# State-space units of a decoder kernel: channel blocks two by two, the scan in place in two PSUM banks, and shares of the work on GpSimd and ScalarE

## What is computed

```python
dt = softplus(dt @ dt_proj_w.T + dt_proj_b)              # per token and channel, 512 channels
dA = exp(einsum('bld,dn->bldn', dt, A))                  # 16 states for each channel
u = einsum('bld,bln->bldn', x, Bc) * dt[..., None]
decay = clip(floor(dA * 2**15), 0.0, 32767.0) / 2**15
h = scan(h = decay * h + u)                              # along the 256 tokens
y = einsum('bldn,bln->bld', h, Cc) + x * D
y = (y * silu(z)) @ out_proj_w.T + out_proj_b
```

## Time and profile before

| | |
|---|---|
| median of 3 runs | 2634.4 us (2625.34 to 2636.75) |
| the profiled execution, its own time | 2631.68 us |
| span of the profiled execution | 2629.8 us |
| DVE busy | 1634.4 us (62%) |
| PE busy | 2168.8 us (82%) |
| ACT busy | 1030.7 us (39%) |
| POOL busy | 289.7 us (11%) |
| units, first scan to last | 1242.6 to 2118.6 us, 128 scans |

### The profile page before, as it was taken

One profiled execution on the slowest core, in us unless ns is written; L12 is line 12 of the kernel. 1 busy time (PEld: TensorE's weight loads), 2 busy tenths in 40 slices (PEclk: granted clock), 3 DMA queues, 4 the chain that ended last, 5 costly groups with the idle time before them and its releaser, 6 DMA issues. The chain is left out here.

```text
span 2629.8 us, 31266 instructions
## 1 busy us (share of the span) xinstructions
PE 2168.8 (82%) x11024; PEld 1327.3 (50%) x11024; DVE 1634.4 (62%) x2717; ACT 1030.7 (39%) x1611; POOL 289.7 (11%) x332
## 2 busy tenths in 40 slices
PE   6999999999999988754668887977888778749994
PEld 4666666666666655431323344434444434536662
DVE  6555555555555566447999999999999952120002
ACT  1222222222222222115765867587668712212220
POOL 1111111111111111100000000010000002110005
PEclk8999999999999999867779987988899876559997
DMA  6000100010001000010110111111001120003333
GB/s 219 1 0 17 46 2 0 17 41 8 0 17 41 7 0 0 1 40 33 54 49 23 47 40 38 34 38 37 27 33 55 48 68 30 15 19 100 100 100 112
DMA packets 57469, 102.55 MB, mean 39 GB/s; under 512 B 7828, under 2 KB 39087, under 8 KB 56832
## 3 DMA queue, kind: packets, MB, share of 16 engines
q1 hardware_dynamic: 54272, 93.67, 10.8%
q0 software_dynamic: 3072, 7.28, 0.9%
HBM read 87.10 MB, written 14.94 MB: 39 GB/s over the span
## 5 line engine op out<-in xcount | busy, mean ns | idle before, releaser
L1788 PE MATMUL pa<-arena 128*128 128x512 f32 x512 | 306.4, 728 | 97.7 <-DVE arena L1363 97.5
L1355 DVE TENSOR_TENSOR_SCAN arena<-arena 128x1024 f32<-128x1024 f32 x128 | 292.3, 2284 | 8.4 <-ACT arena L813 8.0
L1576 PE MATMUL po<-arena 128*128 128x256 f32 x1024 | 230.1, 381 | 0.0
L1566 PE MATMUL pa<-arena 128*128 128x512 f32 x512 | 227.9, 598 | 0.8 <-ACT arena L661 0.8
L1788 PEld LDWEIGHTS pa<-arena 128*128 128x128 f32 x512 | 103.4, 221 | 228.8 <-DVE arena L1363 127.5
L676 ACT COPY arena<-po 128x512 f32<-128x512 f32 x64 | 37.5, 586 | 462.6 <-PE po L1531 462.6
L1576 PEld LDWEIGHTS po<-arena 128*128 128x128 f32 x1024 | 191.2, 189 | 31.9 <-issue 3.5
L528 POOL TENSOR_SCALAR arena<-arena 128x2 f32<-128x2 f32 (+1 forms) x92 | 27.5, 299 | 1602.4 <-DVE arena L1222 932.0
L797 ACT ACTIVATE arena<-arena 128x510 f32<-128x510 f32 x256 | 170.4, 716 | 59.1 <-DVE arena L1355 51.5
L1497 PE MATMUL po<-arena 128*128 128x128 f32 x492 | 94.0, 326 | 117.5 <-ACT arena L824 74.9
L1052 DVE TENSOR_TENSOR arena<-pa,arena 128x512 f32<-128x512 f32 x256 | 158.4, 681 | 25.9 <-PE pa L1511 25.0
(11 more groups left out here) (254 smaller groups left out, 3701.0 us busy)
## 6 DMA issues: line engine op xcount, KB each, us to landing
...
arena<-in_rows SPq DMA_DIRECT2D x8, 256.0 KB, 3.2
```

Of the source, the lines that this page charges most:

```text
L1355: v.tensor_tensor_scan(h.rearrange(flat), decay.rearrange(flat), h.rearrange(flat), 0.0, ALU.mult, ALU.add).then_inc(scan_done, 1)
L1566: last = mm(pa[(i + 2) % 4][:, :], w1[:, k, ts(i, P)], yT[:, k, :], start=k == 0, stop=k == KC - 1)
L1576: last = mm(po[s][:, ts(i, D)], gT[:, c, ts(2 * s + i, P)], w2[:, c, :], start=c == 0, stop=c == FM - 1)
L1788: last = mm(pa[c][:, :], ident, uh[i % len(uh)][:, n, :], start=g == 0 and n == 0, stop=g == NS // NG - 1 and n == NG - 1)
```

## The change

The unit keeps its size, and its work is dealt out anew:

- **Order.** `unit_of` takes the blocks two by two: units 0 to 15 are blocks 0 and 1 with all eight groups, units 16 to 31 are blocks 2 and 3. So a group now lasts two units (`GROUP_UNITS` = 2), and B and C rows are fetched for every two units: 16 times two broadcasts for a pair in place of 8 times two.
- **ACT** keeps the exponentials, now two units ahead. The rounding to integers and back goes. In its place `decay_value` writes the decays into PSUM with two Relu of 512 columns, one for each state, into two banks (`state_banks` = `pa[3]`, `pa[2]`). Each waits until DVE has read that bank's states of the unit before.
- **POOL** rounds the decays in `dA` (a minimum and an addition of 2^8, in one instruction over 1020 columns), and makes u (one product over 1024 columns). The deviations of the next pair's head stand between them, behind units 1, 9 and 22.
- **DVE** scans each bank in place (decays in PSUM, u in SBUF, states into PSUM), and multiplies each by C into `uh`. So a unit is two scans and two products of 512 columns. `drive` goes.
- **Gating** of blocks 0 and 1 is done in units 16 and 17, that of blocks 2 and 3 after the last unit. The sums use two banks (`sum_banks`), and some banks and waits around them change.

```diff
-DECAY_TOP = 1.0 - 2.0 ** -15
-DECAY_STEPS = 2.0 ** 15
-DECAY_MID = DECAY_STEPS - 0.5 - 2.0 ** -9
+DECAY_BELOW_ONE = 1.0 - 2.0 ** -24
+DECAY_SHIFT = 256.0
+DECAY_ROUND = DECAY_SHIFT - 2.0 ** -16
...
+def unit_of(i):
+
+
+    return i // GROUP_UNITS % (NS // NG), i // (UNITS // 2) * 2 + i % 2
...
-    x_banks, z_banks = (pt[0], pa[0], pa[1], pa[2]), (pa[0], pa[2], pt[0], pt[1])
+    x_banks, z_banks = (pt[0], pa[2], pa[0], pa[1]), (pa[0], pa[2], pt[0], pt[1])
+    sum_banks, state_banks = (pa[0], pa[1]), (pa[3], pa[2])
...
-            for g in range(NS // NG):
-                if g == 1:
+            for j in range(UNIT_GROUPS):
+                g = unit_of(GROUP_UNITS * j)[0]
+                if j == 1:
                     sp.wait_ge(dtx_ready, 2 * p + 1)
-                if g >= 2:
-                    sp.wait_ge(hc_ready, UNITS * p + IC * (g - 1))
-                for first, tile in ((0, Bs[g % 2]), (NS, Cs[g % 2])):
-                    sp.dma_start(tile, bc_rows[first + g * NG:first + g * NG + NG, :].partition_broadcast(P)).then_inc(rows_in[g % 2], 16)
-                if g == 2:
+                used = UNITS * p + GROUP_UNITS * (j - 1)
+                if j >= 2:
+                    sp.wait_ge(u_ready, used)
+                sp.dma_start(Bs[j % 2], bc_rows[g * NG:g * NG + NG, :].partition_broadcast(P)).then_inc(b_in[j % 2], 16)
+                if j >= 2:
+                    sp.wait_ge(hc_ready, used)
+                sp.dma_start(Cs[j % 2], bc_rows[NS + g * NG:NS + g * NG + NG, :].partition_broadcast(P)).then_inc(c_in[j % 2], 16)
+                if j == 6:
...
+            if p is not None:
+                for i in range(UNITS):
+                    g, c = unit_of(i)
+                    j = i // GROUP_UNITS
+
+                    if i == 2:
+                        hold(pool, scan_half, UNITS * p + 1)
+                        no_start(dA[2])
+                    hold(pool, grown_ready, UNITS * p + i + 1)
+                    nc.gpsimd.tensor_scalar(past_start(dA[i % len(dA)]), past_start(dA[i % len(dA)]), DECAY_BELOW_ONE, DECAY_ROUND, ALU.min, ALU.add)\
+                        .then_inc(round_ready, 1)
+                    if i in (0, 2):
+                        hold(pool, dtx_ready, 2 * p + 1 + i // 2)
+                    if i % GROUP_UNITS == 0:
+                        hold(pool, b_in[j % 2], 16 * (UNIT_GROUPS // 2 * p + j // 2 + 1))
+                    if i >= len(uh):
+                        hold(pool, ysum_done, UNITS * p + i - len(uh) + 1)
+                    nc.gpsimd.tensor_tensor(uh[i % len(uh)], dtx[:, c, :].unsqueeze(1).broadcast_to([P, NG, W]), Bs[j % 2], ALU.mult)\
+                        .then_inc(u_ready, 1)
+                    if n is not None and i - 1 in STATISTICS:
+                        deviations(GROUPS + groups + STATISTICS.index(i - 1) + 1, 0, TT)
+            elif n is not None:
                 for k in range(3):
                     deviations(GROUPS + groups + k + 1, 0, TT)
...
-                hold(pool, dt_ready, 2 * n + 2)
-                for one in dA:
-                    nc.gpsimd.memset(one.rearrange("p n (s t) -> p (n s) t", s=2)[:, :, 0], 0.0).then_inc(starts_ready, 1)
+                hold(pool, dt_ready, 2 * n + 1)
+                for one in dA[:2]:
+                    no_start(one).then_inc(starts_ready, 1)
...
             def decay_exp(i, p):
-                g, c = i // IC, i % IC
-                if i < IC:
-                    act.wait_ge(dt_ready, 2 * p + 1 + i // 2)
+                g, c = unit_of(i)
+                if i == 0:
+                    act.wait_ge(dt_ready, 2 * p + 1)
+                if i == GATED:
+                    act.wait_ge(dt_ready, 2 * p + 2)
                 if i >= len(dA):
-                    act.wait_ge(scan_done, UNITS * p + i - len(dA) + 1)
+                    act.wait_ge(da_ready, UNITS * p + i - len(dA) + 1)
                 for n in range(NG):
                     last = a_(past_start(dA[i % len(dA)])[:, 2 * n:2 * n + 2, :], dt[:, c, :].rearrange("p (s t) -> p s t", s=2)[:, :, 1:],
                               ACT.Exp, scale=acol[:, c, NG * g + n:NG * g + n + 1])
-                return step.mark(last)
-
-            def decay_steps(i, exped, p):
-
-                step.passed(exped)
-                if i == 0:
-                    act.wait_ge(bc_kept, 16 * p + 16)
-                if i >= 2:
-                    act.wait_ge(da_ready, UNITS * p + i - 1)
-                return step.mark(a_(past_start(steps16[i % 2]), past_start(dA[i % len(dA)]), ACT.Relu, scale=-DECAY_STEPS, bias=const[:, C_MID:C_MID + 1]))
-
-            def decay_value(i, stepped):
-
-                step.passed(stepped)
-                a_(past_start(dA[i % len(dA)]), past_start(steps16[i % 2]), ACT.Copy, scale=-1.0 / DECAY_STEPS, bias=DECAY_TOP).then_inc(da_ready, 1)
+                last.then_inc(grown_ready, 1)
+
+            def decay_value(i):
+
+                act.wait_ge(round_ready, UNITS * p + i + 1)
+                for half in range(NG):
+                    if i:
+                        act.wait_ge((hc_half, hc_ready)[half], UNITS * p + i)
+                    a_(state_banks[half][:, :], dA[i % len(dA)][:, half, :], ACT.Relu, bias=const[:, C_MID:C_MID + 1])\
+                        .then_inc((da_half, da_ready)[half], 1)
...
                 for i in range(UNITS):
-                    if i + 1 < UNITS:
-                        exped = decay_exp(i + 1, p)
-                    if i:
-                        decay_value(i, stepped)
-                    if i + 1 < UNITS:
-                        stepped = decay_steps(i + 1, exped, p)
+                    if i + 2 < UNITS:
+                        decay_exp(i + 2, p)
+                    decay_value(i)
...
-                step.at(ACT_STEPS * n)
-                decay_value(0, decay_steps(0, decay_exp(0, n), n))
+                for i in range(2):
+                    decay_exp(i, n)
...
-            def drive(i):
-
-                g, c = i // IC, i % IC
-                if c == 0:
-                    dve.wait_ge(rows_in[g % 2], 32 * (4 * p + g // 2 + 1))
-                if i >= len(uh):
-                    dve.wait_ge(ysum_done, UNITS * p + i - len(uh) + 1)
-                v.tensor_tensor(uh[i % len(uh)], dtx[:, c, :].unsqueeze(1).broadcast_to([P, NG, W]), Bs[g % 2], ALU.mult).then_inc(u_ready, 1)
+            def scanned(i, half):
+
+                dve.wait_ge((da_half, da_ready)[half], UNITS * p + i + 1)
+                bank = state_banks[half][:, :]
+                v.tensor_tensor_scan(bank, bank, uh[i % len(uh)][:, half, :], 0.0, ALU.mult, ALU.add).then_inc((scan_half, scan_done)[half], 1)
+
+            def read_out(i, half):
+
+                dve.wait_ge((scan_half, scan_done)[half], UNITS * p + i + 1)
+                v.tensor_tensor(uh[i % len(uh)][:, half, :], state_banks[half][:, :], Cs[i // GROUP_UNITS % 2][:, half, :], ALU.mult)\
+                    .then_inc((hc_half, hc_ready)[half], 1)
+
+            def gated(c):
+
+                dve.wait_ge(ysum_done, UNITS * p + (c // 2 + 1) * UNITS // 2 - 1 + c % 2)
+                step.after(v.scalar_tensor_tensor(dtx[:, c, :], xs[:, c, :], skip[:, c:c + 1], sum_banks[c % 2][:, :], ALU.mult, ALU.add))
+                v.tensor_tensor(dtx[:, c, :], dtx[:, c, :], zs[:, c, :], ALU.mult).then_inc(yg_ready, 1)
...
             def unit(i):
 
-                g, c = i // IC, i % IC
-                decay, h = dA[i % len(dA)], uh[i % len(uh)]
-                flat = "p n t -> p (n t)"
-
-                dve.wait_ge(da_ready, UNITS * p + i + 1)
+                j = i // GROUP_UNITS
                 dve.wait_ge(u_ready, UNITS * p + i + 1)
-                v.tensor_tensor_scan(h.rearrange(flat), decay.rearrange(flat), h.rearrange(flat), 0.0, ALU.mult, ALU.add).then_inc(scan_done, 1)
+                scanned(i, 0)
                 if q is not None and i:
                     cross(i - 1)
-                if i + 1 < UNITS:
-                    drive(i + 1)
+                if i in (GATED, GATED + 1):
+                    gated(i - GATED)
+                if i % GROUP_UNITS == 0:
+                    dve.wait_ge(c_in[j % 2], 16 * (UNIT_GROUPS // 2 * p + j // 2 + 1))
+                read_out(i, 0)
+                scanned(i, 1)
                 if n is not None:
                     head(i)
-                dve.wait_ge(scan_done, UNITS * p + i + 1)
-                v.tensor_tensor(h, h, Cs[g % 2], ALU.mult).then_inc(hc_ready, 1)
+                read_out(i, 1)
...
-            if p is not None:
-                dve.wait_ge(dtx_ready, 2 * p + 2)
-                dve.wait_ge(starts_ready, len(dA) * (p + 1))
-                drive(0)
...
-                for c in range(IC):
-                    dve.wait_ge(ysum_done, UNITS * p + UNITS - IC + c + 1)
-                    step.after(v.scalar_tensor_tensor(dtx[:, c, :], xs[:, c, :], skip[:, c:c + 1], pa[c][:, :], ALU.mult, ALU.add))
```

(13 more changed lines are left out.)

52 lines of the change are left out of this document (29 added, 23 removed).

## The result

The changed kernel takes **2741.9 us** (median of 4 runs, 2740.4 to 2745.1) against 2635.6 of the kernel before in the same job: a ratio of 1.041 (95% interval 1.0385 to 1.0431). It is slower by 4%, where the forecast was 2593 us (2548 to 2662), a gain of 42.

A forecast was written before the change was run, and what follows sets the result against it. DVE was taken to bound the units. Its shorter unit (-96), gating (+7), stretch starts (+9), locks (+24) and the small product (+14) sum to -42 us from 2631.7, so 2590, median 2593 us, range 2548 to 2662.

The forecast's parts named there:

- DVE's unit: DVE's two scans and two readouts of 512 columns take 3.70 us where 4.45 stood: 96 us less over 128 units.
- Gating and the start: Gating moved into the stretches costs net +7 us; each stretch's first scan waits for ACT's first bank, +9 us in all.
- POOL's rounding: POOL rounds a decay tile in 1.04 us, at most 2.37, so its 3.4 us unit stays under DVE's 3.70.
- POOL bounds: Rival: POOL's rounding costs as much as a product, its unit takes 4.7 us; +27 us, 2620 us, chance 0.12.
- Locks: DVE instructions without a PSUM operand wait for POOL's instruction: +24 us for head steps and gating, +14 for the small product.
- the small product: Cross attention's 128x2 DVE tensor_scalar (line 1323) waits 2.37 us when behind POOL; 6 of 48 taken as caught, +14 us.
- The race: Small product on DVE starts at 5.46 us, POOL's next u at 5.51, so it is ahead by 0.05 us.
- The covers: ACT's order takes 3.6 us, under DVE's 3.70, and u is ready at 7.88 against 8.2 to 8.5: no time lost.
- Fetches: Fetches of B and C double in number but have two units to land: no time.
- Sums: Rival's total: in-place scans hold POOL off, 7.1 us a unit, +2.6 x 128, 2960 us, chance 0.03.

The follow-up runs named there:

- e3: Changed kernel with POOL's rounding as the addition alone, one operation in place of two: 2706 us, against 2612 for the kernel before (one run).
- e1: Changed kernel with POOL rounding only four columns of a tile, so nearly no rounding: 2660 us, 1.0185 of the kernel before.
- e4: Changed kernel with a POOL copy in place instead of the rounding: 2682 us, against 2612 for the kernel before (one run).
- e7: e1 with a fourth buffer for u and without the cross attention's small product: 1.0065 of the kernel before.
- e14: e10 with ACT's softmax exponentials moved one slot sooner: 0.9985 of the kernel before.
- e10: e7 with PE's transposes of finished heads put ahead of the state sum: 0.9993 of the kernel before.

## Why the prediction was wrong, step by step

**DVE's unit.** Right. Scan 1.22, readout 0.69, quiet step 3.72 where nothing else bounds (3.70 forecast), own work down by 85 us. The scan from and to PSUM takes what was worked out from SBUF scans.

**Gating and the start.** Within the bounds. Passages and first scan together are 9.7 us later, where +9 less 4 of gating's return were put; the first scan alone lies anywhere from 1237 to 1248 us in the traces. Gating's second step was stretched from 0.69 to 1.03 us, as named.

**POOL's rounding: this step failed.** "The rounding is one tile in and one out, so I take 1.04; its upper bound is the product's 2.37." The chosen row is a copy, and a copy does no arithmetic. The bound was taken from the one POOL instruction with more inputs, as if inputs were what costs; it is 3.66. With it POOL's unit is 6.0 us and bounds most of the units that have no head work. The rival "POOL bounds" had this mechanism at 2620 us; with the true price it would have been the main case: 5.90 in 31 steps is 183 us for a stretch, and the first and last were 196 and 188. The rival's own price, 8 us for the first stretch with a POOL unit of 4.7, was low as well: in e3, with 5.04, that stretch is 19 us longer than in e1, which in proportion makes some 14 at 4.7, an estimate. The only POOL tensor_scalar in the rows, line 528, has four columns, and says nothing of a long one. An operation without a row should have had a bound well above the nearest kind. This step is not the whole miss, though. The forecast was 0.984 of before, the kernel came to 1.041, and e4, with the rounding at the forecast's price, to 1.027 (one run). So of some 149 us the price accounts for 37, and 112 were missing with the price right; they are the next two steps.

**Locks.** 24 + 14 us were forecast; 48.5 were measured in the stretches (11.2 the small product, 14.9 the normalisations, 5.3 gating, the rest head steps), a quarter more. Scans and readouts passed POOL untouched, as said. That the 14 for the small product came near is luck. The race was counted with no rounding in POOL's way, and 6 of 48 were to be caught by POOL's product; in the changed kernel 14 are stretched, 4 beside the product and 10 beside the rounding, which the race did not have. Where the rounding is short, more is caught: 17 of 48 both in e4 and in e1, for 20 and 26 us, and all stretched work in e4 is some 64 us.

**The covers.** These are "no time, but with 0.1 to spare" for ACT, and 7.88 against 8.2 for u. This was the second failed step, and the larger one: by e4 most of the 112 us. With the rounding nearly gone DVE is idle for 118 us in e1, 85 more than before. The forecast compared the mean step of each engine. But the loop DVE, ACT, PE, POOL is closed within a unit, since ACT can write a bank only after DVE has read it. So a wait of ACT for PE reaches DVE nearly whole (4.57 us of ACT became 4.07 of DVE in e7's rows, behind a state sum of 3.52 us), where before ACT was a unit ahead. e14's pairs show the same for work of ACT that does not fit its gap. That all of the 85 us come about in this way is argued, not shown. Of the 64 us of new idle time left in e10, 26 stand before the addition of the output (42 against 16 before), where DVE waits for PE itself. How the rest divides between ACT's place, PE's order and PE's clock stays open.

**Fetches.** Right. No engine's waits in the changed kernel's stretches name the B and C rows, though they are fetched twice as often.

**Sums.** One is slightly off: 2.6 x 128 on top of 2634 is 2967, not 2960. Nothing hangs on it.
